# Three PSUM banks for ScalarE and three for VectorE, layer 1 in three rounded passes, and one bank in sixteen moved from VectorE to ScalarE

## The reference

```python
e = stack([tbl_f[ids[:, f]] for f in range(32)], axis=1)       # 512 x 32 x 32
z = einsum('bhd,bmd->bhmd', e, e);    cur1 = relu(einsum('bpd,pn->bnd', z, W0))  # 1024 -> 128 maps
z = einsum('bhd,bmd->bhmd', e, cur1); cur2 = relu(einsum('bpd,pn->bnd', z, W1))  # 4096 -> 128 maps
h = concat([sum_d(cur1), sum_d(cur2), dense_ctx], axis=1)      # 512 x 272
y = relu(relu(h @ W_top1 + b_top1) @ W_top2 + b_top2) @ W_top3 # 512 x 1
```

## Time and profile before

| | us |
|---|---|
| median of 3 runs | 878.09 |
| lowest and highest | 877.87, 881.36 |
| the profiled execution | 877.02 |
| its span, first to last instruction | 875.1 |
| TensorE busy in the span | 855.4 |
| VectorE busy | 797.1 |
| ScalarE busy | 683.0 |
| GpSimd busy | 678.2 |

### The profile page before, as it was taken

The page is one execution under the profiler, slowest core; times in us unless marked ns, Lnnn a source line. Parts: engine busy times, 40 slices in busy tenths (PEclk is TensorE's granted clock), DMA queues, the critical chain, the costliest instruction groups (busy, mean ns, idle before and its releaser), DMA issues.

```text
span 875.1 us, 17350 instructions
## 1 busy us (share of the span) xinstructions
PE 855.4 (98%) x3581; PEld 670.2 (77%) x3581; DVE 797.1 (91%) x2392; ACT 683.0 (78%) x2230; POOL 678.2 (77%) x676
## 2 busy tenths in 40 slices
PE   2999999999999999999999999999999999999998
PEld 2678777777877777787777787777778777778884
DVE  3799999999989999999999999999999998999884
ACT  2588787788888778888778888877888877888883
POOL 5278887879778797979878787887878888786781
DMA  6786666767756676665767656577675676773430
GB/s 184 227 205 144 156 153 140 182 158 158 174 116 156 152 182 157 151 163 109 176 157 177 163 134 156 126 174 166 162 178 116 138 163 165 160 181 76 86 72 1
DMA packets 55486, 131.21 MB, mean 150 GB/s; under 512 B 8101, under 2 KB 19333, under 8 KB 55462
## 3 DMA queue, kind: packets, MB, share of 16 engines
q0 software_dynamic: 22240, 68.17, 42.7%
q1 hardware_dynamic: 31538, 59.99, 21.2%
q10 hardware_dynamic: 1683, 2.80, 1.0%
HBM read 60.67 MB, written 4.20 MB: 74 GB/s over the span
## 4 chain that ended last, share of the span: by engine, by line
PE 95%; DMA 2%; DVE 1%; ACT 0%; POOL 0%; issue 0%; SPq 0%; DVEq 0%; ACTq 0%
PE t_act L721 14%; PE t_dve L721 13%; PE t_act L723 13%; PE t_act L722 13%; PE t_dve L723 13%; PE t_dve L722 13%; PE acc L689 6%; PE acc L694 5%; PE acc_pool L731 1%; PE acc L698 1%; PE acc_pool L733 1%; DMA x_shift<-x_rows 1%; PE acc L675 1%; DVE prod L554 0%; PE t_act L804 0%; POOL emb L249 0%
## 5 line engine op out<-in xcount | busy, mean ns | idle before, releaser
L395 ACT ACTIVATE prod<-t_act,weigh 128x128 f32<-128x128 f32 x2048 | 578.8, 373 | 115.4 <-PE t_act L723 113.6
L543 DVE SCALAR_TENSOR_TENSOR prod<-t_dve,weigh,prod 128x128 f32<-128x128 f32 x1792 | 480.8, 339 | 10.4 <-PE t_dve L723 6.7
L286 POOL TENSOR_TENSOR prod<-prod 128x512 f32<-128x512 f32 (+1 forms) x255 | 320.5, 1257 | 18.5 <-DMA prod<-prod 8.4
L721 PE MATMUL t_act<-w_hi,cur_hi 128*128 128x512 f32 x512 | 215.8, 422 | 0.1
L721 PE MATMUL t_dve<-w_hi,cur_hi 128*128 128x512 f32 x512 | 200.1, 391 | 0.0
L723 PE MATMUL t_act<-w_hi,cur_lo 128*128 128x512 f32 x512 | 199.9, 391 | 0.0
L722 PE MATMUL t_act<-w_lo,cur_hi 128*128 128x512 f32 x512 | 199.9, 390 | 0.0
L723 PE MATMUL t_dve<-w_hi,cur_lo 128*128 128x512 f32 x512 | 199.4, 389 | 0.0
L722 PE MATMUL t_dve<-w_lo,cur_hi 128*128 128x512 f32 x512 | 199.3, 389 | 0.0
L268 POOL DMA_DIRECT2D prod<-prod x126 | 118.5, 941 | 96.6 <-DVE prod L543 73.7
L249 POOL DMA_INDIRECT emb<-table_dram,all_ids x128 | 160.4, 1253 | 34.4 <-issue 23.2
(11 more groups left out here) (85 smaller groups left out, 580.7 us busy)
## 6 DMA issues: line engine op xcount, KB each, us to landing
prod<-prod POOLq DMA_DIRECT2D x126, 512.0 KB, 5.0
x_shift<-x_rows SPq DMA_DIRECT2D x64, 512.0 KB, 6.0
x_pair<-x_rows SPq DMA_DIRECT2D x96, 128.0 KB, 4.4
x_same<-x_rows SPq DMA_DIRECT2D x32, 256.0 KB, 3.4
x_rows<-emb SPq DMA_DIRECT2D x64, 64.0 KB
w_raw<-w_dram ACTq DMA_DIRECT2D x8, 256.0 KB, 5.1
emb<-table_dram,all_ids POOLq DMA_INDIRECT x128, 2.6
w_raw<-wt_dram SPq DMA_DIRECT2D x2, 512.0 KB, 4.7
```

The lines of the kernel that those rows point to most:

```text
L286: nc.gpsimd.tensor_tensor(src[:, dst, :], src[:, dst, :], src[:, other, :], ALU.add).then_inc(folded, 1)
L395: last = nc.scalar.activation(prod[i][:, HEADS * k + j, :], t_act[k % ARING][:, j * MAPS:(j + 1) * MAPS], ACT.Copy, scale=weigh[p][:, i, h ...
L543: nc.vector.scalar_tensor_tensor(dst, src, w, dst, ALU.mult, ALU.add).then_inc(added, 1)
L721: nc.tensor.matmul(bank[:, :], cur_hi[p][:, cols], w_hi[:, w], start=True, stop=False)
```

## The change

- The rings become 3 banks for ScalarE and 3 for VectorE. VectorE's bank number now depends on the chunk modulo 3, so TensorE's and VectorE's loops are written over six chunks (`over_triples`).
- Tiles 0 and 2 give five banks to ScalarE and three to VectorE (`"ADAADADA"`), tiles 1 and 3 four and four (`"ADADADAD"`). A chunk so has 18 and 14 banks in place of 16 and 16. `prod` of tiles 0 and 2 has 20 heads in place of 16: the accumulating DMA moves 10 heads for them, and `fold` has one more addition.
- All four groups of layer 1 are split, so groups 0 and 1 have three fp32r matmuls each in place of one fp32 call. `round_pair` and `lower_pair` are done twice: for groups 2 and 3 where they were, and for groups 0 and 1 of chunk c+2 at the end of chunk c. Chunk 1 keeps fp32 for all four groups, as chunk 0 does.
- `place` moves from VectorE to ScalarE, behind T2. `transpose` moves behind T0. On GpSimd, `halve` goes ahead of the two gathers.
- The head's fourth accumulator is a bank of ScalarE, and all four start only when the last adds are done.

```diff
-DRING, ARING = 4, 2
+ORDER = ["ADAADADA", "ADADADAD"] * (TILES // 2)
+DRING, ARING = 3, 3
...
+FOLDS = {8: [(slice(0, 4), slice(4, 8)), (slice(0, 2), slice(2, 4))],
+         10: [(slice(0, 5), slice(5, 10)), (slice(0, 2), slice(2, 4)), (slice(0, 1), slice(4, 5))]}
...
+        def over_triples(eng, chunk, head=2, tail=6):
+
+            for c in range(head):
+                chunk(c, c % 2, c % DRING)
+            with eng.Fori(0, (CHUNKS - head - tail) // 6) as six:
+                for k in range(6):
+                    chunk(six * 6 + head + k, (head + k) % 2, (head + k) % DRING)
+            for c in range(CHUNKS - tail, CHUNKS):
+                chunk(c, c % 2, c % DRING)
...
 GpSimd, chunk():
-                    if ahead and i < 2:
-                        gather(c + LEAD, (2 * i, 2 * i + 1))
                     here = c == CHUNKS - 1 and i == TILES - 2
                     if not here:
                         halve(c, i)
+                    if ahead and i < 2:
+                        gather(c + LEAD, (2 * i, 2 * i + 1))
...
 ScalarE:
-            def round_pair(c, p):
-                act.wait_ge(z_ready, c * 3 + 3)
-                act.wait_ge(layer1_done, c)
-                nc.scalar.activation(z_hi[:, :, :], z[p][:, WHOLE:GROUPS, :], ACT.Copy).then_inc(pair_rounded, 1)
+            def round_pair(c, p, which):
+
+                g = slice(which * 2, which * 2 + 2)
+                act.wait_ge(z_ready, c * 3 + 1 + 2 * which)
+                act.wait_ge((layer1_half, layer1_done)[which], c - 1 + which)
+                nc.scalar.activation(z_hi[:, g, :], z[p][:, g, :], ACT.Copy).then_inc(pair_rounded, 1)
+
+            def place(c, p):
+
+
+                wait(act, pool2_done, c - 1)
+                nc.scalar.copy(sel[p][:, :], sel_wide[:, bass.ds(c * -QUARTERS + (CHUNKS - 1) * QUARTERS, 128)]
+                               ).then_inc(sel_ready, 1)
...
-                    if i == 0 and not (isinstance(c, int) and c + 1 >= CHUNKS):
-                        round_pair(c + 1, 1 - p)
+                    if i == 0 and not (isinstance(c, int) and (c == 0 or c + 1 >= CHUNKS)):
+                        round_pair(c + 1, 1 - p, 1)
+                    if i == 2:
+                        place(c, p)
+                    if i == 3 and not (isinstance(c, int) and c + 2 >= CHUNKS):
+                        round_pair(c + 2, p, 0)
...
 VectorE, chunk():
+                add_tile(c, 0, p, r)
                 if more1:
                     transpose(c + 1, 1 - p)
-                add_tile(c, 0, p)
-                if more1:
-                    lower_pair(c + 1, 1 - p)
-                place(c, p)
-                add_tile(c, 1, p)
+                if more1 and not (fixed and c == 0):
+                    lower_pair(c + 1, 1 - p, 1)
+                add_tile(c, 1, p, r)
...
-                add_tile(c, 3, p)
+                add_tile(c, 3, p, r)
                 if more2:
                     products(c + 2, p, 1)
+                    lower_pair(c + 2, p, 0)
...
 TensorE, layer1():
-                    if g < WHOLE:
-
-                        if g == 0:
-                            pe.wait_ge(z_ready, c * 3 + 1)
-                        nc.tensor.matmul(acc1[:, :], v[:, g, :], z[p][:, g, :], start=g == 0, stop=False)
...
+                        pe.wait_ge(z_lo_ready, (c - 2) * GROUPS + g + 1)
                         for weights, rows in ((v_hi, z_hi), (v_lo, z_hi), (v_hi, z_lo)):
...
 TensorE, the head:
-                pe.wait_ge(added, (CHUNKS * TILES * HALF - DRING + f + 1) * HEADS)
+                pe.wait_ge(added, CHUNKS * D_CHUNK * HEADS)
+                pe.wait_ge(weighed, CHUNKS * A_CHUNK)
```

More of the change, by code:

```diff
@@ L22 @@
 BANKS = FIELDS // HEADS
-HALF = BANKS // 2
-FEEDS = HALF * HEADS
-DRING, ARING = 4, 2
+ORDER = ["ADAADADA", "ADADADAD"] * (TILES // 2)
+A_BANKS, D_BANKS = ([order.count(who) for order in ORDER] for who in "AD")
+A_BEFORE, D_BEFORE = ([sum(banks[:i]) for i in range(TILES + 1)] for banks in (A_BANKS, D_BANKS))
+A_CHUNK, D_CHUNK = A_BEFORE[TILES], D_BEFORE[TILES]
+DRING, ARING = 3, 3
 SEL_WIDE = 2 * 128 - QUARTERS
@@ L118, in dlrm_tower @@
         t_act = [ps(f"t_act{r}") for r in range(ARING)]
+        t_top = t_dve + t_act[2:]
         acc1 = ps("acc1")
@@ L494, in products, with lower_pair @@
                                             ALU.mult).then_inc(z_ready, 1)
-            def lower_pair(c, p):
-                dve.wait_ge(pair_rounded, c)
-                for k in range(SPLIT):
-                    nc.vector.tensor_tensor(z_lo[:, k, :], z[p][:, WHOLE + k, :], z_hi[:, k, :].bitcast(fp32),
+            def lower_pair(c, p, which):
+                dve.wait_ge(pair_rounded, (c - 2) * 2 + which + 1)
+                for g in (which * 2, which * 2 + 1):
+                    nc.vector.tensor_tensor(z_lo[:, g, :], z[p][:, g, :], z_hi[:, g, :].bitcast(fp32),
                                             ALU.subtract).then_inc(z_lo_ready, 1)
@@ L505, in lower @@
                 dve.wait_ge(cur1_ready, c + 1)
[L507 removed]
+                wait(dve, act_bank, (c - 1) * A_CHUNK)
                 nc.vector.tensor_tensor(
@@ L741, in top_ctx @@
             def top_ctx(f):
-                nc.tensor.matmul(t_dve[f][:, :], wt1_ctx[:, f * 128:(f + 1) * 128], ctx_sb[:, :], start=False, stop=False)
+                nc.tensor.matmul(t_top[f][:, :], wt1_ctx[:, f * 128:(f + 1) * 128], ctx_sb[:, :], start=False, stop=False)
             pe.wait_ge(wh_ready, HEADS)
@@ L774, in _ @@
             for f in range(T1):
-                pe.wait_ge(added, (CHUNKS * TILES * HALF - DRING + f + 1) * HEADS)
+                pe.wait_ge(added, CHUNKS * D_CHUNK * HEADS)
+                pe.wait_ge(weighed, CHUNKS * A_CHUNK)
                 rows = slice(f * 128, (f + 1) * 128)
                 for w, x in ((wt1_hi, pool1_hi), (wt1_lo, pool1_hi), (wt1_hi, pool1_lo)):
-                    nc.tensor.matmul(t_dve[f][:, :], w[:, 0, rows], x, start=w is wt1_hi and x is pool1_hi, stop=False)
+                    nc.tensor.matmul(t_top[f][:, :], w[:, 0, rows], x, start=w is wt1_hi and x is pool1_hi, stop=False)
             top_ctx(0)
@@ L796, in pool2_upper @@
                 for w in (wt1_hi, wt1_lo):
-                    nc.tensor.matmul(t_dve[f][:, :], w[:, 1, f * 128:(f + 1) * 128], pool2_hi, start=False, stop=False)
+                    nc.tensor.matmul(t_top[f][:, :], w[:, 1, f * 128:(f + 1) * 128], pool2_hi, start=False, stop=False)
             def h1_upper(k):
@@ L812, in _ @@
             for f in range(T1):
-                nc.tensor.matmul(t_dve[f][:, :], wt1_hi[:, 1, f * 128:(f + 1) * 128], pool2_lo, start=False,
+                nc.tensor.matmul(t_top[f][:, :], wt1_hi[:, 1, f * 128:(f + 1) * 128], pool2_lo, start=False,
                                  stop=True).then_inc(top1_done, 1)
```

152 lines of the change are left out of this document (78 added, 74 removed).

## The result

The changed kernel takes 912.61 us (median of 4 runs, 906.82 to 916.49), beside 878.05 us for the kernel before on the same chip. The ratio is 1.037, with a 95% interval of 1.033 to 1.0409: slower by 34.6 us, and above the range given. The profiled execution is the longest of the four, 916.49 us with a span of 914.6, so its trace shows 39.5 us more span than that of before.

The account below looks back on a forecast made before the run. TensorE's queue was taken as the bound. 877.0 us minus 30 x (25.79 - 25.56) = 6.9, plus 0.6, gave 870.7; with 1.1 for the median, 871.8, say 872. The 8-in-10 range was 864 to 896.

Parts of the forecast that it names:

- What TensorE saves: TensorE, chunks 2 to 31: six fp32r matmuls, 1.36 us, replace the 1.72 us fp32 call, 0.36 a chunk.
- Loop 1: ScalarE through VectorE to TensorE's last T3 bank: a new stall of 0.26 us a chunk, period 25.48.
- bare queue: TensorE's slots alone: 111 x 0.2267 = 25.16 us a chunk, against 25.79.
- Loop 2: VectorE's queue from T3's first add round to TensorE's last T1 bank: 23.8 us plus B.
- B: Time VectorE is held up by GpSimd in loop 2, at the new lower_pair: up to 1.9 us, once.
- a sign of being wrong: GpSimd without idle time ahead of its T3 halve, which would make GpSimd the bound.
- the 1.7 that are free: Slack in loop 2: B costs nothing up to 25.48 - 23.8 = 1.7 us.
- rival 2: GpSimd holds up both halves of the new lower_pair: period 26.2 to 26.6, 891 to 903 us; chance 0.33.
- Rival 3: A wash: lower2, between T2 and T3, held up in half the chunks; 874 to 882 us; chance 0.24.
- the instruction which comes first wins: VectorE instructions with two SBUF inputs and GpSimd's SBUF reads exclude each other for a whole instruction; the first wins.
- The start: First chunks: larger roundings hidden; later gathers put SP's rows some 2.5 us back, products wait a whole chunk later.
- The tail: Head's first matmul waits for the last add: 1.1 us later, 0.5 covered, cost 0.6 us.

Follow-up runs that it names:

- e15: Changed kernel with four-and-four tiles, rings 4 and 2, place ahead of relu1, gathers first in chunks 0 and 1 only: 868.95 us, ratio 0.9869.
- e18: e15 with halve ahead of the gathers in the first two chunks too: 872.31 us, ratio 0.9903 to the kernel before.
- e7: e1 without GpSimd's fold additions, except the last of each tile: 878.25 us, ratio 0.9965 to the kernel before.
- e1: Changed kernel with VectorE's and TensorE's loops of six chunks written out, every instruction the same: 910.4 us, ratio 1.0295 to the kernel before.
- e5: Changed kernel with four-and-four tiles, 3 banks for VectorE and 2 for ScalarE, a spare head bank, loops written out: 933.14 us, ratio 1.0599.
- e8: e1 with GpSimd's gathers ahead of halve, as before the change: 894.24 us, ratio 1.0141 to the kernel before.
- e13: e1 without the additions of GpSimd's fold of T2, except the last: 890.09 us, ratio 1.0123 to the kernel before.
- e17: Changed kernel with VectorE's loop of six running from chunk 4 to 28 in place of 2 to 26: 905.68 us, ratio 1.0259.
- e4: Kernel before, with VectorE's and TensorE's loops over six chunks in place of two: 885.25 us, ratio 1.0042.
- e16: e2 with the first chunk of VectorE's loop moved from 2 to 4: 923.83 us, ratio 1.0501 to the kernel before.
- e12: e8 with VectorE alone in the loop of six chunks, TensorE still written out: 936.91 us, ratio 1.0654 to the kernel before.
- e2: Changed kernel with rings of 4 banks for VectorE and 2 for ScalarE, and loops of two chunks again: 1021.51 us, ratio 1.1574.

## Why the prediction was wrong

**What TensorE saves: right.** Six slots in place of the fp32 call show once nothing else binds: steps of 25.37 in e15 and e18, against 25.79. The bare queue was given as 25.16.

**Loop 1: right.** Predicted a stall of 0.26 once a chunk, `place` at 0.26, a step of 25.48. Measured in the chunk at 457.74: a wait of 0.3, 0.19 and 25.40; in e7, where nothing is held up, 25.44.

**Loop 2: the step that failed.** It was, in the prediction's words, "The place where the new `lower_pair` goes looks the same", and then "I take B up to 1.9 once". The ordinary steps of the changed kernel are 26.25 in the mean, not 25.56. In e1's chunk shown the fold of T2 starts 19.4 us behind the start of T2 on TensorE (594.25 and 574.82), where it started 15.5 behind it before (446.02 and 430.53). It is 3.9 us later and meets the old pair, one place further on in VectorE's queue. I had placed GpSimd's folds by where they stood in the trace of before, although the change adds 2.5 us a chunk to GpSimd ((757.3 - 678.2) / 32; the prediction's own loads had 1.8 of them). Its slack shows ahead of T3's `halve`, in the kernel before and in e1:

```profile
445.43 0.86 POOL L268 DMA_DIRECT2D prod<-prod  x1 [3.56 <-DVE prod L543]
```

```profile
593.08 0.88 POOL L277 DMA_DIRECT2D prod<-prod  x1
```

The idle time there has gone, which the prediction had listed as a sign of being wrong.

The sum of loop 2 itself holds once the hold-ups are read from where they are. B is what products 1 (1.21 alone) and the two pairs (1.28 each alone) take longer, plus a wait of the old pair for `round_pair`, which the sum didn't have:

| chunk | held up | B | 23.8 + B | step |
|---|---|---|---|---|
| changed kernel, 156.34 | old pair 3.20, wait 0.46 | 2.38 | 26.18 | 26.12 |
| changed kernel, 208.52 | products 1 2.88, new pair 2.09, old pair 1.52 | 2.72 | 26.52 | 26.38 |
| changed kernel, 775.47 | products 1 2.84, new pair 2.08, old pair 1.52 | 2.67 | 26.47 | 26.40 |
| e1, 574.59 | old pair 3.23, wait 0.42 | 2.37 | 26.17 | 26.18 |
| changed kernel, 457.74 | old pair 2.38, wait 0.22 | 1.32 | 25.12 | 25.40 |

In the last of them B is under the 1.7 that are free, and loop 1 has the step. So it is rival 2, which gave 26.2 to 26.6 at a chance of 0.33: its sign and size were right, its place (the new pair) was so in some chunks only, and it had left out products 1. Rival 3's mechanism, a late `lower2`, is seen in e5, e8 and e13, and in four of the changed kernel's own chunks (2.72 us in the one at 509.38).

What isn't separated is GpSimd's own queue. In e1's chunk it waits for a transfer for 0.3 us and stands still for 1.5 more between its gathers, so the hold-ups fill it too. That ScalarE and VectorE don't wait for GpSimd's results in such a chunk, and that the sums fit, speaks for loop 2. One more thing in the prediction's rows doesn't fit its reading that the instruction which comes first wins: L564 starts 0.08 before GpSimd's addition and is the one that takes 1.55 longer. So the recorded starts don't tell which of two will wait.

**Not in the prediction at all: the loop's returns.** 16.6 us. The edit to loops over six chunks had been listed and costed at nothing. e1 and e17 take the gaps away with no other change, and give 1.0295 and 1.0259 in place of 1.037: less than 16.6 us, since e1's trace has another long step, and e17's starts 5.1 us later.

**The start: wrong, 7.8 us.** "The later gathers put SP's rows some 2.5 us back; products wait for them a whole chunk later" holds in the middle, not in the first two chunks, where products wait for these rows directly. How much of it is the order of gathers and `halve` isn't settled. Between e8 and e1 the first start moves by 4.8 us. But e17 and the changed kernel execute the same instructions up to there, and their starts are 82.16 and 77.04, so two executions can differ by that much for another reason. Over all runs, gathers first has 69.79 to 79.14 with a mean of 72.9 (six kernels), and `halve` first has 71.84 to 82.16 with a mean of 77.1 (twelve). The x_shift transfer on that chain took 8.60 us in e18 and 11.51 in the changed kernel, and in the latter TensorE's first slots behind the wait were 0.43 us, so a longer wait is paid twice. Before, two `halve` transfers of 512 KB (issued at 42.83 and 46.71) overlapped it too. What sets the transfer's length was not settled.

**The tail: 3.1 against 0.6.** TensorE's head waits 1.88 us for the last adds. In the other kernels the same stretch is 58.0 (e4) to 63.6 us (e16); e18 and e15, both with the head started bank by bank, have 58.1 and 61.3, so the head's start doesn't explain it. This stays open.

**What also stays open** is why a return costs 5 to 10 us in one place and nothing in another. The Trainium skill, "Runtime: NRT & Kernel Launch", section "Instruction fetch mechanics", says that a taken branch to a block of instructions that is no longer held makes the sequencer fetch it first. The gaps look like that, and e16 and e17 show that the loop's place in the stream decides. But e17 has the same loop body as the changed kernel, the same 52 packets in the instruction queue and no gap, which the rule alone doesn't explain.

## What to carry to other kernels

When a change adds work to an engine that is off the critical path, don't reuse the positions of its instructions from the trace of before: work out how late it will be, and then what it will meet. Count a PSUM ring as the slack that absorbs another engine's hold-ups: here the fourth bank was worth 2.0 us in a chunk with a hold-up of 1.9, while the trace of before shows only 0.8 us of waits for VectorE in all, and so doesn't show what it hid. A loop rewritten over more iterations is an edit with a price of its own; look for "issue" gaps at its returns, and if there are some, try another first iteration before another length. And compare the start of two executions of the same code before giving a difference there to an edit.

## What the runs showed of the hardware that was not expected

- A return of VectorE's loop left the engine idle for 5 to 6 us (changed kernel), up to 9.5 (e12) and up to 10.5 (e2). The same loop moved by two chunks left no gap (e16, e17).
- After a wait of 3.71 us in the middle of the kernel, TensorE's matmuls came 0.43 us apart for 3.5 us, then 0.2267 again. Eight slots with 0.2 us each make the stall cost some 1.6 us more than its length. It was so at all three returns: 11 slots at the second, and seven at the third, behind the first few short ones.
- A `halve` transfer of 640 KB lands in 6.1 us in the median; one in e1 took 9.8 (issued at 749.79), so that GpSimd waited 5.25 us for it, in a step that was 7.4 us longer than the others (33.61 against 26.17).
- VectorE's 128x512 subtraction takes 689 ns without GpSimd's additions (e7) and 1024 in the mean with them (e1). It goes both ways: in e1's chunk shown GpSimd's two additions for T1 take 3.94 us beside products 1 and the new pair, where the earlier trace rows have 2.40.
